# Folding norm, rotation and transposes of a local-attention layer into the loops around them, with work moved to ScalarE and GpSimd

## The reference

```python
def _layer(x, wqkv, qs, ksc, wo, lg, lb, w1, b1, w2, b2):
    h = shift_token(x)                      # half of the features from one token earlier
    q, k, v = jnp.split(h @ wqkv, 3, axis=-1)   # 1024 -> 3 x 512, 8 heads of 64
    q = l2norm(q) * qs                      # per token and head
    k = l2norm(k) * ksc
    q, k = rotary_xpos(q, k)                # x * cos * scale + rotate_half(x) * sin * scale
    o = local_attention(q, k, v)            # window of 512 keys back, softmax
    x = x + o @ wo
    ...                                     # LayerNorm, w1, a * gelu(g), w2, residual
```

## Time and profile before

| | us |
|---|---|
| median of 3 runs (lowest, highest) | 4952.22 (4950.34, 5043.11) |
| the profiled execution, its own time | 4950.34 |
| its span on the slowest core (core 7), first to last instruction | 4948.8 |
| spans of the 8 cores | 4919.7 to 4948.8 |
| mean granted TensorE clock of the cores | 0.702 to 0.703 of full speed |

### The profile page before, as it was taken

One profiled execution on the slowest core, in us unless ns is written; L12 is line 12 of the kernel. 1 busy time (PEld: TensorE's weight loads), 2 busy tenths in 40 slices (PEclk: granted clock), 3 DMA queues, 4 the chain that ended last, 5 costly groups with the idle time before them and its releaser, 6 DMA issues.

```text
span 4948.8 us, 41528 instructions; the slowest of 8 cores (4919.7 to 4948.8 us)
## 1 busy us (share of the span) xinstructions
PE 2869.4 (58%) x12144; PEld 1205.4 (24%) x12144; DVE 1469.0 (30%) x3038; ACT 1314.0 (27%) x2021; POOL 65.1 (1%) x112
## 2 busy tenths in 40 slices
PE   2564566767687044444639878732344447587962
PEld 1220012222233012222304333311122231233421
DVE  5365330000013842222251101266222225211112
ACT  1102125656530013333213122000334331220300
POOL 0000000000000000000000000000000000000000
PEclk9975567777788555555769989875555558798985
DMA  2301120000012000000025152100000000523324
GB/s 61 56 1 55 33 45 20 20 20 18 15 65 46 0 1 1 1 1 1 9 35 80 23 92 45 43 1 1 1 0 1 1 9 0 92 45 58 57 73 153
DMA packets 100669, 157.56 MB, mean 32 GB/s; under 512 B 14906, under 2 KB 67772, under 8 KB 99434
## 3 DMA queue, kind: packets, MB, share of 16 engines
q0 software_dynamic: 69952, 82.83, 10.6%
q1 hardware_dynamic: 30508, 72.08, 4.7%
HBM read 208.35 MB, written 29.36 MB: 48 GB/s over the span
## 4 chain that ended last, share of the span: by engine, by line
PE 50%; DVE 19%; ACT 12%; issue 10%; DMA 7%; DVEq 1%; ACTq 0%; SPq 0%; POOL 0%; POOLq 0%
PE P L1635 7%; PE P L1580 6%; PE P L1572 6%; PE P L502 4%; ACT pn L1303 4%; DVE misc L1299 4%; PE P L904 3%; PE P L1352 3%; PE P L856 3%; PE P L1284 3%; DMA w1g<-w 3%; PE P L930 3%; PE P L1114 2%; ACT ptf L228 2%; ACT ptb L870 2%
## 5 line engine op out<-in xcount | busy, mean ns | idle before, releaser
L1352 PE MATMUL P<-ptf,v_tok 128*64 128x128 bf16 x1120 | 165.0, 307 | 675.2 <-ACT ptf L228 392.6
L1572 PE MATMUL P<-hln,w1a 128*128 128x512 bf16 (+1 forms) x1408 | 341.1, 386 | 176.5 <-DMA w1a<-w 176.5
L1303 ACT ACTIVATE pn<-P,misc 128x640 bf16<-128x640 f32 (+4 forms) x256 | 186.2, 727 | 875.9 <-DVE misc L1299 875.7
L870 ACT ACTIVATE ptb<-P,misc 128x1024 bf16<-128x1024 f32 (+7 forms) x384 | 321.9, 864 | 136.5 <-PE P L856 82.2
L1580 PE MATMUL P<-hln,w1g 128*128 128x512 bf16 (+1 forms) x1408 | 337.7, 383 | 10.2 <-DMA w1g<-w 10.2
L1299 DVE TENSOR_REDUCE misc<-P 128x1 f32<-128x640 f32 (+4 forms) x256 | 189.7, 741 | 473.1 <-PE P L1330 471.1
L1352 PEld LDWEIGHTS P<-ptf,v_tok 128*64 128x64 bf16 x1120 | 111.8, 159 | 735.7 <-issue 735.7
L1602 DVE TENSOR_TENSOR mid<-asc,glu 128x512 bf16<-128x512 bf16 (+1 forms) x176 | 74.8, 425 | 679.4 <-ACT glu L1596 679.4
L1590 ACT ACTIVATE asc<-P,lt_g 128x512 bf16<-128x512 f32 (+1 forms) x176 | 121.0, 688 | 568.5 <-PE P L1572 568.5
L904 PE MATMUL P<-ptb,v 128*65 128x512 bf16 (+3 forms) x640 | 231.9, 436 | 34.4 <-DVE attnT L940 34.2
L940 DVE TENSOR_TENSOR attnT<-P,bcn_sb 64x1024 bf16<-64x1024 f32 x32 | 39.0, 1218 | 673.9 <-ACT bcn_sb L935 673.9
(11 more groups left out here) (201 smaller groups left out, 3727.3 us busy)
## 6 DMA issues: line engine op xcount, KB each, us to landing
w1a<-w POOLq DMA_DIRECT2D x20, 1024.0 KB, 9.3
w1g<-w POOLq DMA_DIRECT2D x20, 1024.0 KB, 13.6
w2a<-w POOLq DMA_DIRECT2D x4, 2816.0 KB, 21.4
w2b<-w POOLq DMA_DIRECT2D x4, 2560.0 KB, 15.6
xstage<-x SPq DMA_DIRECT2D x16, 512.0 KB, 3.4
s_scratch<-s_stage SPq DMA_DIRECT2D x32, 256.0 KB, 2.8
s_ld<-s_scratch SPq DMA_DIRECT2D x8, 1024.0 KB, 5.0
x_ld<-x SPq DMA_DIRECT2D x16, 512.0 KB, 4.1
```

The lines of the kernel that those rows point to most:

```text
L870: ex = p.s(lambda e, pt=pt, off=off, lspan=lspan, pb=pb: e.activation(out=pt_sb[pb][:, 0:lspan], in_=pt[:, off:off + lspan], func=AF.Exp, ...
L1303: t_ex = p.s(lambda e, scp=scp, sco=sco, nk=nk, m3=m3, mc=mc: e.activation(out=pn_sb[m3][:, 0:nk], in_=scp[:, sco:sco + nk], func=AF.Exp, ...
L1352: stop=(r == 3 and i == ntr - 1): e.matmul(otp[0:64, oto + r * 128: oto + r * 128 + 128], v_tok[:, kt * 512 + h * 64: kt * 512 + h * 64 + 64],
L1572: sla=sla, hlo=hlo: e.matmul(sla[0][0:wdt, sla[1]:sla[1] + 512], w1a[jj][:, k * gw + mi * 128: k * gw + mi * 128 + wdt], hln[:, k * T + hl ...
```

## The change

- The bf16 casts of `y`: chunks 0 to 4 stay on VectorE, chunks 5 to 7 go to GpSimd, ahead of the issue of the `wqkv` load in GpSimd's list.
- The four scaled tables are computed before the QKV loop instead of after it.
- The copies of q, k and v out of PSUM go from VectorE to ScalarE. Norm and rotation are done inside the QKV loop, tile by tile: squares on ScalarE (f32 scratch of two halves), sums and clamp on VectorE, Ln and Exp on ScalarE over 16 columns, now 16 times each; the sine product goes to GpSimd; the sum is bf16 instead of f32; the product with the norm takes a bf16 norm and writes back into `q_tok` and `k_tok`.
- The barriers between QKV, tables, norm, rotation, transposes and attention are gone.
- The transposes go into the attention loop: before each of the four blocks `w4`, those of its four tiles. The four transposes of a tile of q (or k) share one PSUM bank of `P3` and one copy of 128x512, by ScalarE for q and by VectorE for k.
- The row buffer of `stage_param_tiles` is split in two, and its first DMA waits for the last copies of `q_feat` and `k_feat`.

```diff
         for c in range(NCH):
-            tok_ybf.append(p.v(lambda e, c=c: e.tensor_copy(out=ybch(c), in_=ych(c)),
+            eng = p.v if c < 5 else p.g
+            tok_ybf.append(eng(lambda e, c=c: e.tensor_copy(out=ybch(c), in_=ych(c)),
                                waits=y_ready + tok_ybg))
...
-            e1 = p.v(lambda e, tt=tt, ptq=ptq, offq=offq: e.tensor_copy(
+            e1 = p.s(lambda e, tt=tt, ptq=ptq, offq=offq: e.copy(
                 out=q_tok[:, tt * 512:(tt + 1) * 512], in_=ptq[:, offq:offq + 512]),
                 waits=[qm])
...
+            sq_q = p.s(lambda e, tt=tt: e.activation(
+                out=sqf[:, 0:512], in_=q_tok[:, tt * 512:(tt + 1) * 512],
+                func=AF.Square, bias=0.0, scale=1.0), waits=[e1, sqf_war[0]])
+            red_q = p.v(lambda e, tt=tt: e.reduce_sum(
+                out=ss[:, tt * 16: tt * 16 + 8], in_=vap(sqf, 0, [(64, 8), (1, 64)]),
+                axis=AX.X), waits=[sq_q])
...
+            t_cl = p.v(lambda e, tt=tt: e.tensor_scalar(
+                out=ss[:, tt * 16: tt * 16 + 16], in0=ss[:, tt * 16: tt * 16 + 16],
+                scalar1=1e-24, scalar2=None, op0=ALU.max), waits=[red_q, red_k])
+            t_l1 = p.s(lambda e, tt=tt: e.activation(
+                out=ss[:, tt * 16: tt * 16 + 16], in_=ss[:, tt * 16: tt * 16 + 16],
+                func=AF.Ln, bias=0.0, scale=1.0), waits=[t_cl])
+            t_rs = p.s(lambda e, tt=tt: e.activation(
+                out=ssb[:, tt * 16: tt * 16 + 16], in_=ss[:, tt * 16: tt * 16 + 16],
+                func=AF.Exp, bias=0.0, scale=-0.5), waits=[t_l1])
+            for ti, (srcb, ctab, stab, sq_war) in enumerate(
+                    [(q_tok, cqs, sqs, sq_q), (k_tok, cks, sks, sq_k)]):
+                etok = tok_qkv[tt][ti]
+                a1 = p.v(lambda e, srcb=srcb, ctab=ctab, tt=tt: e.tensor_tensor(
+                    out=vap(r1, 0, [(64, 8), (1, 64)]),
+                    in0=vap(srcb, tt * 512, [(64, 8), (1, 64)]),
+                    in1=vap(ctab, tt * 64, [(0, 8), (1, 64)]), op=ALU.mult),
+                    waits=[etok] + tok_tab)
+                a2 = p.g(lambda e, srcb=srcb, stab=stab, tt=tt: e.tensor_tensor(
+                    out=vap(r2, 0, [(64, 8), (32, 2), (1, 32)]),
+                    in0=vap(srcb, tt * 512 + 32, [(64, 8), (-32, 2), (1, 32)]),
+                    in1=vap(stab, tt * 64, [(0, 8), (32, 2), (1, 32)]), op=ALU.mult),
+                    waits=[etok, last_a3[0]] + tok_tab)
+                a3 = p.v(lambda e: e.tensor_tensor(out=r3[:, :], in0=r1[:, :], in1=r2[:, :],
+                                                   op=ALU.add), waits=[a1, a2])
+                last_a3[0] = a3
+                prevt = p.v(lambda e, srcb=srcb, tt=tt, ti=ti: e.tensor_tensor(
+                    out=vap(srcb, tt * 512, [(64, 8), (1, 64)]),
+                    in0=vap(r3, 0, [(64, 8), (1, 64)]),
+                    in1=vap(ssb, tt * 16 + ti * 8, [(1, 8), (0, 64)]), op=ALU.mult),
+                    waits=[a3, t_rs, sq_war])
+                rot_tok[(ti, tt)] = prevt
...
+        def emit_transposes(tq):
+            for ti, (srcb, dstb) in enumerate([(q_tok, q_feat), (k_tok, k_feat)]):
+                tpo = 512 * ((2 * tq + ti) % 2)
+                b = bank_of(P3, tpo)
+                ptv = P3[:, tpo: tpo + 256].bitcast(BF16)
+                ttr = None
                 for dc in range(4):
...
+                    ttr = p.t(lambda e, srcb=srcb, tq=tq, dc=dc, ptv=ptv,
+                              start=(dc == 0), stop=(dc == 3): e.matmul(
+                        ptv[:, dc * 128:(dc + 1) * 128],
+                        srcb[:, tq * 512 + dc * 128: tq * 512 + dc * 128 + 128],
+                        id_bf[:, :], start=start, stop=stop, is_transpose=True),
+                        waits=([rot_tok[(ti, tq)], tok_idbf] + pw_waits([b]))
+                        if dc == 0 else [])
+                pw_done([b], ttr)
+                eng = p.s if ti == 0 else p.v
+                ev = eng(lambda e, dstb=dstb, tq=tq, ptv=ptv: _EngShim(e).tensor_copy(
+                    out=vap(dstb, tq * 128, [(T, 4), (1, 128)]), in_=ptv[:, 0:512]),
+                    waits=[ttr])
+                pr_done([b], ev)
...
+        for w4 in range(4):
+            for tq in range(w4 * 4, w4 * 4 + 4):
+                emit_transposes(tq)
+            for h in range(8):
+                for r in range(4):
+                    fq.append(ffn_emit_A(idx, h, w4, r))
+                    idx += 1
+                    if len(fq) > 4:
+                        ffn_emit_B(fq.pop(0))
```

More of the change, by code:

```diff
@@ L1141, in ffn_layer @@
-        if dbg_stop == "qkv":
-            return ("DBG", [("dbg_q", q_tok), ("dbg_k", k_tok), ("dbg_v", v_tok)],
-                    [t[0] for t in tok_qkv] + [t[1] for t in tok_qkv] + [t[2] for t in tok_qkv])
-        ar.free(f"wqkv{l}")
-        ar.free(f"y_bf{l}")
-        p.barrier()
-        q_rot = ar.alloc(f"q_rot{l}", [128, NTT * 512], BF16)
-        k_rot = ar.alloc(f"k_rot{l}", [128, NTT * 512], BF16)
         cqs = ar.alloc(f"cqs{l}", [128, NTT * 64], BF16)
@@ L1166, in ffn_layer @@
                 waits=tok_qs + tok_xp))
+        wqkv_sb = ar.alloc(f"wqkv{l}", [128, 8 * 1536], BF16)
+        tok_wqkv = p.gdma(lambda e: e.dma_start(
+            out=vap(wqkv_sb, 0, [(1536, wqkv_sb.shape[1] // 1536), (1, 1536)]),
+            in_=W["wqkv"][l].rearrange("(c p) m -> p c m", p=128)), chain=f"wqkv{l}")
+        q_tok = ar.alloc(f"q_tok{l}", [128, NTT * 512], BF16)
+        k_tok = ar.alloc(f"k_tok{l}", [128, NTT * 512], BF16)
+        v_tok = ar.alloc(f"v_tok{l}", [128, NTT * 512], BF16)
@@ new lines, in ffn_layer @@
+        ss = ar.alloc(f"ss{l}", [128, NTT * 16], F32)
+        ssb = ar.alloc(f"ssb{l}", [128, NTT * 16], BF16)
+        sqf = ar.alloc(f"sqf{l}", [128, 2 * 512], F32)
+        r1 = ar.alloc(f"r1_{l}", [128, 512], BF16)
+        r2 = ar.alloc(f"r2_{l}", [128, 512], BF16)
+        r3 = ar.alloc(f"r3_{l}", [128, 512], BF16)
+        qk_ps = [(P2, 0), (P1, 1024)]
+        v_ps = [(P1, 0), (P1, 512)]
+        tok_qkv = []
+        sqf_war = [None, None]
+        last_a3 = [None]
+        rot_tok = {}
@@ L1167, in ffn_layer @@
+        if dbg_stop == "qkv":
+            return ("DBG", [("dbg_q", q_tok), ("dbg_k", k_tok), ("dbg_v", v_tok)],
+                    [t[0] for t in tok_qkv] + [t[1] for t in tok_qkv] + [t[2] for t in tok_qkv])
+        if dbg_stop == "rot":
+            return ("DBG", [("dbg_q", q_tok), ("dbg_k", k_tok)],
+                    [rot_tok[kk] for kk in rot_tok])
+        ar.free(f"wqkv{l}")
+        ar.free(f"y_bf{l}")
         for n in ("xcq", "xsq", "xck", "xsk"):
             ar.free(n + str(l))
-        p.barrier()
@@ L1185, in ffn_layer @@
-        t_cl = p.v(lambda e: e.tensor_scalar(out=ss[:, :], in0=ss[:, :], scalar1=1e-24,
-                                             scalar2=None, op0=ALU.max), waits=tok_ss)
-        t_l1 = p.s(lambda e: e.activation(out=ss[:, :], in_=ss[:, :], func=AF.Ln,
-                                          bias=0.0, scale=1.0), waits=[t_cl])
-        t_rs = p.s(lambda e: e.activation(out=ss[:, :], in_=ss[:, :], func=AF.Exp,
-                                          bias=0.0, scale=-0.5), waits=[t_l1])
@@ L1219, in ffn_layer @@
-        ar.free(f"r1_{l}")
-        ar.free(f"r2_{l}")
-        ar.free(f"r3_{l}")
-        ar.free(f"q_tok{l}")
-        ar.free(f"k_tok{l}")
-        ar.free(f"ss{l}")
-        p.barrier()
         q_feat = ar.alloc(f"q_feat{l}", [128, 4 * T], BF16)
```

192 lines of the change are left out of this document (66 added, 126 removed).

## The result

The changed kernel takes 4678.75 us in the median of 12 executions (4641.26 to 4822.61); the kernel before, on the same chip, 4955.16 us. The ratio is 0.9396, with a 95% interval of 0.9352 to 0.9439: 6% faster, some 299 us.

What follows compares the result with a forecast made beforehand. The kernel was taken as a sequence of stages, each with its own limit. Per layer 108.9 + 26 + 3 = 137.9 us replace 279.5 and 280.9, saving 284.6 from 4950.3: 4666 us predicted, range 4608 to 4745.

Steps and rivals of the forecast that it cites:

- The loop: Fused QKV loop, first matmul to last rotation: 16 tiles at 6.2 us plus the first tile's start, 108.9 us per layer.
- ScalarE's round trip: QKV loop: ScalarE's next copies stand behind Ln, which waits for the clamp; 5.05 us clamp to clamp, just under TensorE's pace.
- VectorE alone at 5.6 us: QKV loop, per tile: VectorE's sums, clamp and two rotations take 5.6 us, a little slower than TensorE's 5.18.
- half a turn: QKV loop: VectorE waits between nothing and 1.2 us per tile for GpSimd's product; middle taken, giving 6.2 us per tile.
- Rival 2: QKV loop: VectorE and GpSimd take turns at memory, 6.9 us per tile, 11.2 more per layer; 4688 us, chance 0.26.
- Rivals 3 and 6: GpSimd near memset price, 7.8 us per tile, late weight load: 4765, chance 0.08; GpSimd's per-element price, slower than before: 5068, 0.02.
- Before the loop: Start of each layer's QKV stage: GpSimd's casts ahead of the weight load make it late, +3 us per layer.
- a third of the transfer's time for the tables beside it: Weight load before the loop: with the tables going first, the transfer alone needs two thirds of 24.1 us.
- Transposes: In the attention loop: about 1.45 us per tile, 6.5 us per block, 26 us for four blocks per layer.
- Rival 4: Attention loop: blocks of transposes drain the pipeline at every boundary, 55 us instead of 26; 4724 us, chance 0.06.
- rival 5: Attention: it comes in with a warm TensorE and keeps the full clock, 150 to 164 us saved; 4510 us, chance 0.03.
- Rival 1: QKV loop: TensorE keeps the pace, 5.4 us per tile, 12.8 us less per layer; 4640 us, chance 0.22.

Runs made afterwards that it cites:

- the long write: Changed kernel with GpSimd's sine product of k replaced by a write of 1024 contiguous elements that reads nothing, k's sine part left out; a turn of 5.18 us.
- the short write: Changed kernel with GpSimd's sine product of k replaced by a memset of 256 separate elements, k's sine part left out; a turn of 5.18 us.
- experiment 6: Changed kernel with all 16 tiles' transposes ahead of attention instead of four tiles before each block; transposes 21.9 us beyond the loop, attention 614.7 us.
- edit 1: Changed kernel with the sine product of k back on VectorE, q's staying on GpSimd; ratio to before 0.9342, a turn of 5.26 us.

## Why the prediction was right

The forecast was 4666 us, in a range from 4608 to 4745; the measured median is 4678.75, and 0.9396 of 4952.2 would be 4653. The five shortest executions take 4641 to 4649 us, near the 4950.3 - 306 = 4644 that the stages give, so the nearness of the median to 4666 is in part luck. The prediction was right in its total and in what it named as the owner of each stage. But two of its three terms came out by errors that cancel, and a reader should not take the total for a proof of the parts.

**The loop: 108.9 predicted, 105.4 measured; 6.2 us per tile against 6.0.** VectorE does own it (52.35 of 60 us in its middle), ScalarE's round trip does not (Ln waits 2.96 us for the clamp, with ScalarE idle). The step that failed is VectorE alone at 5.6 us. The starts in the turn shown add up to 5.97 us, of which the norm product of q holds 1.67 - 0.69 = 0.98 waiting; that leaves 5.0. I had given every operation the spacing of dependent ones, but where the next one does not need the result it starts before the end. The two sums are 0.59 apart and not 0.79; the clamp I had at 0.35, and the cosine product starts 0.09 behind its start; and what follows a norm product starts 0.61 behind it and not 0.80 (1563.16 to 1563.77; 1566.42 to 1568.02 less the 0.98). That is 0.20 + 0.26 + 0.37 = 0.83 too many, against 0.2 too few for the cosine products and the sums of the rotation (0.53 to 0.60 apart, taken at 0.52). With 5.0 us VectorE would be below TensorE's 5.18, and the long write shows that loop: 5.18 us, TensorE busy for 60.00 of 60 us.

The second step was how VectorE and GpSimd share memory. I took half a turn, 0.6 us, between nothing and 1.2; measured is 0.98 per tile over VectorE's 5.0, or 0.82 over the pace of TensorE that the loop would have had, 13 us per layer. Rival 2 had the mechanism and the wrong base: in turn it is, but from 5.0 and not from 5.6, so 6.0 and not 6.9 us. Splitting a question that has two answers down the middle gave a good number and no knowledge.

**GpSimd's prices.** The sine product, taken at 1.2, is 1.15 us where nothing holds it. The 1.1 us that the prediction scaled as an estimate from the 4497 ns in the page GPSIMD Engine Reference of the Trainium skill, section 3.1, agree with this trace. The casts, taken at 4.8 us, are 1.89 us (2048 elements, one tensor read). The memset of 1.236 us was no measure for either: the same number of separate elements took 385 ns in the short write. Rivals 3 and 6, which lived from that row, were far off.

**Before the loop: +3 predicted, +2.4 and +1.6 measured.** Here two errors cancel. The lines of core 7 that answer to the earlier trace rows:

```profile
1478.90 5.56 POOL L1095 CAST y_bf<-y 128x2048 bf16<-128x2048 f32 x3 [0.39 <-POOL y_bf L1043]
...
1484.42 0.88 POOL L1117 DMA_DIRECT2D wqkv<-wqkv  x1
...
1489.22 5.77 DVE L1095 CAST y_bf<-y 128x2048 bf16<-128x2048 f32 x5 [0.36 <-issue]
```

```profile
1506.52 1.01 PE L1143 MATMUL P<-wqkv,y_bf 128*128 128x512 bf16 x2 [18.00 <-DMA wqkv<-wqkv]
```

The load is issued 6.2 us after the first memset and not 15, since the casts are short; but it does not profit from the tables having gone first. It lands after 21.1 us (18.9 to 23.1 on cores 0 and 7 in both layers) and not after two thirds of 24.1 = 16. That step, a third of the transfer's time for the tables beside it, failed: with the engines to itself the load still takes 21.1 us, against 25.1 us beside the tables in the kernel before (core 7, layer 0). What TensorE waits for is the load, as predicted, and VectorE's casts and tables are through 7 us earlier. I had overlooked that VectorE would start sooner too: the scale rows, no longer behind the load, let its casts begin 11.0 us after the first memset and not 17.9 (1489.22 and 1508.15, from 1478.2 and 1490.3).

**Transposes: 26 predicted, 18.3 measured by the attention of before** (3.9 + 14.4 on core 7, where the attention took 616.1 us before and 630.5 after), 19.7 by the attention of experiment 6 (3.9 + 15.8). The mechanism was right and the size too high: 1.45 us per tile against 1.32 to 1.37, and the first block costs 3.9 us beyond the loop instead of 6.5, because its first transposes are done while VectorE still rotates the last tile. With the loop this is the main part of the 22 us by which the stages gained more than predicted (306 against 284.6). Rival 4, a drained pipeline at 55 us, is out by experiment 6.

**What was given nothing.** Attention kept its clock of 0.50, so rival 5 is out. The four tables lie ahead of the first matmul. The loop's clock is 1.00 in its middle (1540 to 1600 us), as the earlier trace rows let expect at 84% busy. Rival 1, TensorE's pace, is what the changed kernel would have done without the waiting, and what edit 1 does to within 0.08 us. Of ScalarE's function table the trace shows one reload of 1.28 us in the two loops (L1188, layer 1), and the kernel before has one at the same place (L1187).

**A sign that did not hold.** VectorE was to be busy for over 80% of the stretch to the first score; it was for 83.89 + 1.24 of 109.3 us, 78%. My own terms, 16 x 5.6 of 115 us, gave 78% too: the sign was set against the sum.

## What to carry over

Before work goes from VectorE to GpSimd, look at what VectorE will be doing at that moment: an operation that reads two tensors from SBUF and a GpSimd operation that reads even one take turns, while reductions and GpSimd's writes do not mind. Give GpSimd the piece with time to spare and leave the piece that VectorE waits for where it is: moving one product back made a loop with more VectorE work faster. And when a forecast hits, check its terms one by one, since here 5.6 + 0.6 and 5.0 + 1.0 gave the same turn.

## What the runs showed of the hardware

- VectorE's product of two bf16 tensors of 512 elements takes 0.69 us alone and 1.67 us when a GpSimd product of 1.15 us starts 0.03 us ahead of it; 1.54 us behind a copy of 1.04 us. GpSimd's own product takes 1.67 instead of 1.15 us when it starts 0.04 us behind VectorE's. The second waits and is not slowed throughout: it ends 0.54, 0.55 and 1.02 us after the first, each some 0.14 us less than its length alone.
- GpSimd: 1.15 us for a product of 512 bf16 elements, 1.04 us for a bf16 copy of 1024, 1.89 us for a cast of 2048 from f32 to bf16, 0.95 us for a write of 1024. A write of 256 separate elements took 385 ns in the loop and 1.236 us in the kernel before; why, no run here shows.
- VectorE starts an independent operation 0.09 us before the end of a 0.68 us sum (1563.77 to 1564.36), and a dependent one 0.10 us after it (1564.36 to 1565.14).
- A load of 3 MB (f32 in HBM, bf16 in SBUF) takes 21.1 us from issue to landing behind four tables of 512 KB, with the DMA engines to itself, and 26.2 us when it is issued 5.6 us earlier, beside them. The DMA engines are busy for 87 and 89% of the two stretches.
